# Splitting the first batch's load into three pieces, and two one-element activations placed ahead of their tables' first users

## The reference

```
q, k, v = x @ Wq.T + bq, x @ Wk.T + bk, x @ Wv.T + bv      # split in 16 heads
q = softmax(q, over the 16 channels of a head);  k = softmax(k, over the 1024 tokens)
out = q @ (k.T @ v);   out = layernorm(out) * ln_g + ln_b
x = layernorm(x + out @ Wo.T + bo)
h = layernorm(x) @ ternary(w1).T + b1;   h = gelu(h);   h = layernorm(h)
x = layernorm(x + h @ ternary(w2).T + b2)
```

## Time and profile before

| | us |
|---|---|
| median of 3 runs | 580.91 |
| the profiled execution's own time | 580.7 |
| its span, first to last instruction | 578.6 |
| TensorE busy | 544.4 |
| VectorE busy | 498.7 |
| ScalarE busy | 477.4 |
| GpSimd busy | 397.9 |
| first matmul starts at | 11.04 |

### The profile page before, as it was taken

How to read it: one execution, slowest core, us unless ns; L and a number is a source line. 1 busy time by engine, 2 the same in 40 slices (tenths; PEclk the granted TensorE clock), 3 DMA queues, 4 the chain that set the end, 5 groups by cost and what they waited for, 6 DMA issues and landing times.

```text
span 578.6 us, 10831 instructions
## 1 busy us (share of the span) xinstructions
PE 544.4 (94%) x3536; PEld 493.5 (85%) x3536; DVE 498.7 (86%) x1280; ACT 477.4 (83%) x935; POOL 397.9 (69%) x385
## 2 busy tenths in 40 slices
PE   2989999999999999999899999999999999999990
PEld 2889998999898999989689888888898888889890
DVE  3898788887878888876668899999999999999986
ACT  3461779897877987787989999999999999999983
POOL 0563879769597976658748868666767766675772
PEclk9999999999999999989999999999999999999996
DMA  5632022050613203043110012221122222010002
GB/s 179 257 120 74 2 103 118 1 219 2 227 65 136 85 11 136 1 170 124 73 38 2 37 74 74 75 73 38 38 74 74 73 75 74 33 42 37 38 38 109
DMA packets 11399, 46.52 MB, mean 80 GB/s; under 512 B 1360, under 2 KB 1744, under 8 KB 9168
## 3 DMA queue, kind: packets, MB, share of 16 engines
q1 hardware_dynamic: 11344, 45.83, 21.9%
HBM read 29.02 MB, written 16.81 MB: 79 GB/s over the span
## 4 chain that ended last, share of the span: by engine, by line
PE 56%; ACT 6%; POOL 5%; DVE 4%; issue 3%; ACTq 0%; POOLq 0%; DVEq 0%
PE ring L1767 20%; PE qps_sps_aps_then_y L1791 20%; PE qps_sps_aps_then_y L1640 6%; PE qps_sps_aps_then_y L1657 3%; PE ring L1709 2%; PE ring L1583 1%; ACT zjunk L682 1%; PE qps_sps_aps_then_y L1565 1%; PE ring L1722 1%; ACT z L690 1%; POOL xt L410 1%; POOL xc_lo L389 1%; ACT ring L733 1%; PE ring L1684 1%; PE ring L1672 1%
## 5 line engine op out<-in xcount | busy, mean ns | idle before, releaser
L1791 PE MATMUL qps_sps_aps_then_y<-ff_w_over_xc_lo,ff_a_lo_over_qw 128*128 128x258 f32 x512 | 126.3, 283 | 0.0
L1791 PE MATMUL qps_sps_aps_then_y<-ff_w_over_xc_lo,ff_a_hi_over_xc_lo 128*128 128x258 f32 x512 | 126.2, 283 | 0.0
L1767 PE MATMUL ring<-ff_ht_hi_over_qw,t 128*128 128x512 f32 x256 | 106.0, 414 | 2.0 <-DVE ff_sums L1219 1.0
L1767 PE MATMUL ring<-ff_ht_lo_over_xc_hi,t 128*128 128x512 f32 x256 | 101.1, 395 | 0.0
L1791 PEld LDWEIGHTS qps_sps_aps_then_y<-ff_w_over_xc_lo,ff_a_hi_over_xc_lo 128*128 128x128 f32 x512 | 96.8, 189 | 3.5
L1791 PEld LDWEIGHTS qps_sps_aps_then_y<-ff_w_over_xc_lo,ff_a_lo_over_qw 128*128 128x128 f32 x512 | 96.6, 189 | 3.4
L1180 DVE SCALAR_TENSOR_TENSOR ff_a_lo_over_qw<-ring,ff_rho,ff_a_hi_over_xc_lo 128x512 fp32r<-128x512 f32 x128 | 91.5, 742 | 7.8 <-ACT ff_a_hi_over_xc_lo L751 6.9
L733 ACT ACTIVATE ring<-ring,bias 128x512 f32<-128x512 f32 x128 | 84.1, 675 | 11.7 <-PE ring L1767 10.3
L503 POOL TENSOR_TENSOR ff_accp_over_xt_lo<-ff_accp_over_xt_lo,ff_sq_over_ek_et_hi 128x512 f32<-128x512 f32 x64 | 84.0, 1313 | 11.5 <-ACT ff_sq_over_ek_et_hi L749 7.0
L749 ACT ACTIVATE ff_sq_over_ek_et_hi<-ring 128x512 f32<-128x512 f32 x128 | 78.8, 615 | 0.5
L751 ACT CAST ff_a_hi_over_xc_lo<-ring 128x512 fp32r<-128x512 f32 x128 | 77.6, 606 | 0.0
(11 more groups left out here) (172 smaller groups left out, 1617.0 us busy)
## 6 DMA issues: line engine op xcount, KB each, us to landing
x_scratch<-z SPq DMA_DIRECT2D x16, 514.0 KB, 3.0
ff_x_over_w_raw_xc<-x_scratch SPq DMA_DIRECT2D x16, 514.0 KB, 4.8
xt<-in_x_tok_dram SPq DMA_DIRECT2D x8, 1024.0 KB, 4.8
out_dram<-ff_z_over_et_lo SPq DMA_DIRECT2D x15, 512.0 KB, 3.5
xc<-in_x_chan_dram SPq DMA_DIRECT2D x7, 1024.0 KB, 6.9
w_raw<-in_w_dram SPq DMA_DIRECT2D x2, 1024.0 KB, 5.6
xc<-in_x_chan_dram SPq DMA_DIRECT2D x2, 512.0 KB, 5.9
out_dram<-ff_z_over_et_lo SPq DMA_DIRECT2D x2, 256.0 KB, 2.7
```

What stands on the lines that cost most here:

```text
L1767: mm = nc.tensor.matmul(ff_bank(k, m), t1[:, c, m * P:(m + 1) * P], h[:, k % 2, c], start=(c == 0 and j == 0), stop=(c == CH - 1 and j == 1))
L1791: last = nc.tensor.matmul(ff_yps[:, t, 0:C + 2], a[:, m % DEPTH, t * P:(t + 1) * P], ff_w2[:, m], start=(m == 0 and j == 0), stop=(m == FC ...
```

## The change

Three things change.

1. Batch 0's channels come in pieces of 256, 256 and 512 tokens instead of twice 512. Each piece has its own load, its own cast on ScalarE and its own subtraction on VectorE. `q_product(0, 0)` now waits for the first piece alone (`first_lo_ok`); the later two count on `xc_lo_ok`, so its total, and with it the wait of `chan_load(1)` for 2, is what it was.
2. ScalarE computes the exponential of one element per partition (`warm`, 128x1) before it waits for the first piece. The first table load moves with it.
3. ScalarE computes the gelu of one element per partition right behind `k_exponent(7, 1)`, the last exponential of the program. The second table load moves there from `ff_gelu(0, 0)`.

```diff
+        warm = sb("warm", [P, 1])
...
+        FIRST = (slice(0, 2 * P), slice(2 * P, HALF), slice(HALF, N))
...
-            for h in range(2):
-                sp.dma_start(xc[:, :, h * HALF:(h + 1) * HALF], x_chan[0][:, :, h * HALF:(h + 1) * HALF]
-                             ).then_inc(first_in[h], 16)
+            for n, some in enumerate(FIRST):
+                sp.dma_start(xc[:, :, some], x_chan[0][:, :, some]).then_inc(first_in[n], 16)
...
             act.wait_ge(half_ok, 6)
-            for h in range(2):
-                half = slice(h * HALF, (h + 1) * HALF)
-                act.wait_ge(first_in[h], 16)
-                nc.scalar.copy(xc_hi[0][:, :, half], xc[:, :, half]).then_inc(first_hi_ok, 1)
+            nc.scalar.activation(warm[:], nhalf[:, 0:1], ACT.Exp).then_inc(warm_ok, 1)
+            for n, some in enumerate(FIRST):
+                act.wait_ge(first_in[n], 16)
+                nc.scalar.copy(xc_hi[0][:, :, some], xc[:, :, some]).then_inc(first_hi_ok, 1)
...
             k_exponent(NB - 1, 1)
+            act.wait_ge(warm_ok, 1)
+            nc.scalar.activation(warm[:], nhalf[:, 0:1], ACT.Gelu).then_inc(warm_ok, 1)
             product_out(NB - 2, 2)
...
-            for h in range(2):
-                half = slice(h * HALF, (h + 1) * HALF)
-                dve.wait_ge(first_hi_ok, h + 1)
-                split_lo(xc_lo[0][:, :, half], xc[:, :, half], xc_hi[0][:, :, half]).then_inc(xc_lo_ok, 1)
+            for n, some in enumerate(FIRST):
+                dve.wait_ge(first_hi_ok, n + 1)
+                split_lo(xc_lo[0][:, :, some], xc[:, :, some], xc_hi[0][:, :, some]
+                         ).then_inc(xc_lo_ok if n else first_lo_ok, 1)
...
                 if b == 0:
-                    pe.wait_ge(xc_lo_ok, 1 + v // 2)
+                    if v == 0:
+                        pe.wait_ge(first_lo_ok, 1)
+                    else:
+                        pe.wait_ge(xc_lo_ok, (v + 1) // 2)
```

More of the change, by code:

```diff
@@ L206, in both_halves @@
         bq_in, rows_in = sem("bq_in"), sem("rows_in")
-        first_in = [sem(f"first_in{h}") for h in range(2)]
+        first_in = [sem(f"first_in{n}") for n in range(3)]
+        first_lo_ok = sem("first_lo_ok")
         first_hi_ok = sem("first_hi_ok")
+        warm_ok = sem("warm_ok")
         w_in = [sem(f"w_in{n}") for n in range(4)]
```

## The result

The changed kernel takes 582.09 us, median of 20 executions (580.8 to 583.49); the kernel before, timed beside it, 580.98 (579.96 to 582.44). The ratio is 1.0018, with a 95% interval of 1.001 to 1.0025: about 1.1 us slower, less than the 0.3% that was set as the bound of "no change". The forecast was 581.0, so the range held the time and its likeliest case did not: its own range ended at 581.7, and the time lies between it and rival B (582.4 to 583.0), which had a chance of 0.10. The profiled execution took 582.89 us with a span of 580.7, against 580.7 and 578.6 before.

A forecast was written before the change was run, and what follows sets the result against it. The prediction took TensorE to set the pace between two gaps. From the profiled execution's 580.7 us, -1.0 at the start and +1.2 at the seam gave 580.9, forecast as 581.0, range 579.5 to 582.6.

The forecast's parts named there:

- its likeliest case: Whole kernel: start gain and seam loss nearly equal, 581.0 us, own range 580.1 to 581.7; chance 0.54.
- rival B: Wait before q_product(1, 0): clock falls to 1.2 GHz behind it, costing some 1.5 us, 582.4 to 583.0; chance 0.10.
- The start's mechanism: Batch 0: hidden load and smaller pieces start TensorE earlier, then it waits for batch 1's xc_lo; gain 1.0 us.
- rival C: Batch 1's load chain does not bind, so TensorE's 2.3 to 2.9 us come through: 579.3 us; chance 0.09.
- the landing of the third piece: Batch 0's last piece lands at 8.5 us if bytes count, 9.1 if packets count.
- A loss is excluded: Start: no loss unless the third piece lands over 1.8 us later than the half did.
- The seam: Second table load ahead of product_out(6, 2): attend(6, 4) comes 1.2 us late, and this goes through to the end.
- Rival D: Second table load takes longer at its new place, up to 1.3 us more: 581.1 to 582.2; chance 0.07.
- The lower price of a one-element activation: Early gelu on ScalarE at the seam: taken as 0.1 us, since the operation has one column.
- the clock holds in the 2 us gap: Wait before q_product(1, 0): the forecast added no cost for a slower clock behind about 2 us of waiting.
- two equal terms: Start gain of 1.0 us and seam loss of 1.2 us nearly cancel, leaving +0.2 us.

The follow-up runs named there:

- e2: The kernel before with only the one-element gelu added behind the last exponential; 582.4 us, ratio 1.0015 to the kernel before.
- e3: The kernel before with only the one-element exponential added at the start, halves kept; 580.16 us, ratio 0.998 to the kernel before.
- e8: The kernel before with the one-element exponential and VectorE making the second half of batch 1's xc_lo; 581.6 us, ratio 1.0004 to the kernel before.
- e6: The changed kernel without the early gelu, VectorE making the second half of batch 1's xc_lo instead of GpSimd; 580.64 us, ratio 0.9986 to the kernel before.
- look_a: The changed kernel unaltered, first of three further profiled executions; 581.89 us.
- e1: The changed kernel without the one-element gelu, so the second table load is back at the first gelu; 581.33 us, ratio 1.0007 to the kernel before.
- e7: The changed kernel with the one-element gelu moved behind pt_high(7, 3), where ScalarE waits anyway; 581.11 us, ratio 1.0 to the kernel before.
- e4: The kernel before with the three pieces alone, neither one-element activation; 580.77 us, ratio 0.9994 to the kernel before.
- e5: The changed kernel without the gelu, with nine 128x512 matmuls filling TensorE's wait for batch 1; 581.2 us, ratio 0.9998 to the kernel before.
- e9: The changed kernel without the gelu, with two pieces of 256 and 768 tokens instead of three; 581.47 us, ratio 0.9999 to the kernel before.

## Why the prediction was right, and where it was wrong

**The start's mechanism was right, its gain too large.** The table load is hidden, TensorE starts at 7.53 (forecast 8.2 to 8.8), batch 0 is 2.6 us ahead and all of it ends in the wait for `xc_lo`; rival C is refuted by the 1.99 us gap with GpSimd as its releaser. The term was 1.0 us. The changed kernel starts `q_product(1, 0)` at 23.11, 23.71, 23.59 and 23.57, against 23.91 before and 24.18 in e2, whose start is the same code: 23.50 against 24.04 on average, 0.55 us. The step that was mis-sized is the landing of the third piece. I weighed 8.5 (bytes) against 9.1 (packets) and took a value near the bytes; its cast starts at 9.01, 9.64, 9.42 and 9.49. Against the second half's 8.46 in e3 and 8.69 in e8 that is 0.3 to 1.2 us late, out of the 1.28 that the load gives. The low parts end at 11.32, 11.94, 11.73 and 11.79, where the forecast had 10.8 to 11.4. "A loss is excluded" rested on a wrong sum as well: by its own terms, 8.5 + 1.04 + 1.22 = 10.76 against 12.03, the gain is used up when the third piece lands 1.3 us late and not 1.8, and in e6 it was (cast at 9.83, low part's end at 12.13). Alone, the load gives 1.3 at the start (e3: 22.63) and 1.2 in the kernel's time.

**The seam was right.** Forecast 1.2 us late from 1.5 less 0.3 of slack; the gap is 1.22, 1.20, 1.22 and 1.21 us in the four profiles of the change, 1.00 in e2, and the part grows by 1.1 (look_a) and 1.3 (e2). Rival D is refuted: the accumulator read ahead of the load ends at 262.55, the load starts at 262.57, 262.57 + 1.28 = 263.85, and the gelu starts at 263.86. The Trainium skill, ScalarE: Activation LUTs, section "What ACT_TABLE_LOAD costs", puts a drain of 1.38 us on top of the load; the trace disagrees, with 0.01 us here. The lower price of a one-element activation was right: it takes 0.20 us, and the next starts 0.11 behind it.

**The step that failed is "the clock holds in the 2 us gap".** I gave B 0.10 because the nearest row had a gap of 1.67 us with full-speed matmuls behind it, and let that gap speak for 2.1 us. Behind gaps of 1.67 us ahead of the `ek` transposes the clock held in 13 of 13 profiles of this study. Behind those of 1.92 to 2.08 us it fell in 4 of 7: in the changed kernel in 3 of 4, and once in e6, at its 2.06 us; it held in look_a, e1 and e7. The price of 1.5 us was about right: the part is 1.6 to 1.8 us longer than in look_a, each time at 0.50 or 0.51 for some 3.4 us. There is a third length: the gap that ends between 278 and 283 us, released by VectorE's `r_f`, is 1.84 to 1.85 us long in e1, e4, e5, e6 and e7, and the clock fell behind it in e1, e6 and e7; where it is 1.60 to 1.63 us (before, e3, e8, e9) or 1.16 to 1.17 (e2 and the change) it held. So 1.67 us told little of 2.1. Nor does the wait alone tell it: the profile of the kernel before has the fall at 253 with no wait over 0.49 us ahead of it, and the forecast, which looked at waits alone, missed it. B was neither sure nor small: it differs between executions of the same code, and should have had about half of the weight.

The Trainium skill, TensorE: Matmul & The Clock Gate, section "Part 1: The HAM clock gate (the "warmup" mystery)", has an idle array fall back to 1.2 GHz; the traces agree that this happens, and show it behind 2 us only in part of the executions.

**The new sum**, from profiles: -0.55 at the start, +1.1 at the seam, and some 1.7 for the clock in 3 of 4, about +1.3: +1.8 us. The medians give 1.1, which this sum would meet if the clock fell in a third of the executions, (1.1 + 0.55 - 1.1) / 1.7; how often it does without a profile isn't seen. The parts by themselves give nearly the same: e1 (the start without the seam) 1.0007 and e2 (the seam without the start) 1.0015 make 1.0022 against 1.0018. So at the end the seam cost 0.9 of the 1.2 us that it was priced at, and the start, priced at a gain of 1.0, gave none that can be told from zero. That e1 and e7 are no faster than before in their medians, though their profiles start `q_product(1, 0)` 0.7 and 1.2 us early, has its counterpart in the 0.8 us that the fall at 281 took in both. In the profile of e5 the clock falls only at 252, where it costs next to nothing; why its median is no better than e1's, and the spread of e8, stay open.

The shares of faster, same and slower (0.12, 0.74, 0.14) put most on "same", and that is what was measured; the reason given for it, two equal terms, is borne out only by look_a, the one profile of the changed kernel in which the clock stayed up behind the gap (581.89, with a start worth 0.2 to 0.5 us). That the time is "same" and in the range is in part luck: both were wide enough to hold a start that gained nothing, and B's fall of the clock in most of the profiles.

## What to carry to other kernels

Hide a table load where the engine is idle and nobody waits for what comes next: at the start it gave 1.2 us, ahead of a copy with 0.3 us of slack it took about 1. An earlier start is worth only what the next slow link takes over: follow the last piece, not the first, and price the gap that opens where the gain ends, since TensorE may come out of 2 us of waiting at half its clock. When a change is made of parts, time each alone and together: here one line gave the whole gain (0.998), the pieces did no harm alone (0.9994) and undid it when added to that line (1.0007), and the early gelu cost some 0.9 us more.

## What the runs showed of the hardware that was not expected

The clock's fall behind a gap is not decided by the gap alone: the same code with 1.97 to 2.08 us of waiting kept 1.00 in one execution and went to 0.50 or 0.51 in three, twice at the gap's end and once 1.3 us later. It also falls without a long gap: in 6 of 14 profiles at 252.0 to 253.7 us, with waits of no more than 0.5 us ahead of it. The landing of a transfer may depend on what is behind it in its queue: the first 256 KB were there for the cast at 5.5 to 6.1 us in eight profiles with a piece of 256 KB behind them, and at 7.45 in the one profile with 768 KB behind; one profile does not show the cause. GpSimd's subtraction of 128x1024 went from 2.4 to 3.37 us, in e6 and e8 alike, when VectorE made the like beside it for 1.23 us.
